# Selective scan in a four-layer token tower: the D*xc term moved to TensorE, four side jobs moved from VectorE to GpSimd and ScalarE

## The reference, cut to what matters

```
xc    = silu(conv(x_in) + conv_b)                       # 128 channels x 1024 steps
sel   = xc @ sel_w.T  ->  dt_in, Bm (16), Cm (16)
dt    = softplus(dt_in @ dt_w.T + dt_b)
dA_n  = exp(dt * A_n)          dBu_n = dt * xc * Bm_n
h_n   = dA_n * h_n(previous step) + dBu_n               # a scan along the 1024 steps
y     = sum over n of (h_n * Cm_n)  +  D * xc
out   = (y * silu(z)) @ out_w.T
```

## Time and profile before

| | |
|---|---|
| the profiled execution's own time | 1573.16 us |
| its span, first to last instruction | 1571.4 us |
| median of three runs | 1578.91 us |
| mean granted TensorE clock | 0.959 of full speed |
| TensorE busy | 1370.2 us, 87% |
| VectorE busy | 1079.3 us, 69% |
| ScalarE busy | 689.0 us, 44% |
| GpSimd busy | 415.8 us, 26% |

### The profile page before, as it was taken

One profiled execution on the slowest core, in us unless ns is written; L12 is line 12 of the kernel. 1 busy time (PEld: TensorE's weight loads), 2 busy tenths in 40 slices (PEclk: granted clock), 3 DMA queues, 4 the chain that ended last, 5 costly groups with the idle time before them and its releaser, 6 DMA issues. The chain is left out here.

```text
span 1571.4 us, 16757 instructions
## 1 busy us (share of the span) xinstructions
PE 1370.2 (87%) x5750; PEld 564.0 (36%) x5770; DVE 1079.3 (69%) x1253; ACT 689.0 (44%) x979; POOL 415.8 (26%) x242
## 2 busy tenths in 40 slices
PE   6877899988987779999997778999999777899897
PEld 2222233346422223325632222332563222333265
DVE  3598956674559995667455998556746699765673
ACT  0455543334245554324425554532541655543344
POOL 3256610012006660002100766000300276500040
PEclk9989999998999999999898999999989899999997
DMA  8100020000000002000000000200000000020000
GB/s 255 72 0 1 1 57 11 1 1 1 14 0 0 1 1 67 2 1 1 1 14 0 0 1 0 68 1 1 1 1 14 0 0 1 4 51 1 0 2 14
DMA packets 24692, 26.02 MB, mean 17 GB/s; under 512 B 4610, under 2 KB 21794, under 8 KB 24098
## 3 DMA queue, kind: packets, MB, share of 16 engines
q1 hardware_dynamic: 24002, 20.61, 4.5%
q10 hardware_dynamic: 608, 4.34, 0.9%
HBM read 20.73 MB, written 4.21 MB: 16 GB/s over the span
## 5 line engine op out<-in xcount | busy, mean ns | idle before, releaser
L405 POOL TENSOR_TENSOR scratch<-scratch 128x1024 f32<-128x1024 f32 x124 | 306.1, 2468 | 467.3 <-ACT scratch L872 312.1
L1081 DVE TENSOR_TENSOR_SCAN scratch<-ps,scratch 128x1024 f32<-128x1024 f32 x128 | 292.2, 2283 | 5.5 <-ACT ps L865 5.5
L551 PE MATMUL ps<-scratch,consts 128*128 128x512 f32 x512 | 255.6, 622 | 14.0 <-ACT work L896 12.0
L416 POOL TENSOR_TENSOR work<-work,rmax 128x512 f32<-128x512 f32 x64 | 67.4, 1053 | 614.3 <-DVE rmax L1231 614.3
L865 ACT ACTIVATE ps<-steps,vec 128x1024 f32<-128x1024 f32 x128 | 143.1, 1118 | 183.4 <-DVE scratch L1081 183.4
L1133 DVE TENSOR_TENSOR scratch<-scratch,ps 128x1024 f32<-128x1024 f32 x108 | 131.9, 1221 | 117.8 <-PE ps L610 114.8
L905 ACT ACTIVATE scratch<-ps 128x1024 f32<-128x1024 f32 x108 | 108.8, 1022 | 177.3 <-PE ps L597 177.3
L1073 DVE TENSOR_TENSOR scratch<-steps,ps 128x1024 f32<-128x1024 f32 x128 | 156.1, 1219 | 24.4 <-PE ps L525 16.3
L525 PE MATMUL ps<-bc,pick 128*128 128x512 bf16 x244 | 78.7, 402 | 98.6 <-DVE scratch L1073 97.5
L597 PE MATMUL ps<-h_odd,w 64*128 64x512 f32 x512 | 141.6, 639 | 3.8 <-ACT scratch L905 3.8
L610 PE MATMUL ps<-scratch,w 64*128 64x512 f32 x512 | 134.9, 602 | 8.1 <-DVE scratch L1133 8.1
(11 more groups left out here) (194 smaller groups left out, 1626.9 us busy)
## 6 DMA issues: line engine op xcount, KB each, us to landing
steps<-routed_table SPq DMA_DIRECT2D x128, 64.5 KB, 1.9
decayT<-in_decayT SPq DMA_DIRECT2D x8, 512.0 KB, 19.3
work<-in_table ACTq DMA_DIRECT2D x1, 2064.0 KB, 12.6
routed_table<-work SPq DMA_DIRECT2D x1, 2064.0 KB, 8.1
w<-in_w ACTq DMA_DIRECT2D x4, 512.0 KB, 19.5
out<-h_even SPq DMA_DIRECT2D x4, 512.0 KB, 2.6
bc<-in_x_next SPq DMA_DIRECT2D x3, 512.0 KB, 3.6
bc<-in_x_first SPq DMA_DIRECT2D x1, 512.0 KB, 4.5
```

The source lines that it names most:

```text
L405: pool.tensor_tensor(hc_slot(k), hs_slot(k), c_slot(k), ALU.mult).then_inc(sem["hc_ready"], 1)
L551: m = mm(ps[:, 6 + c, :], ident, hc_slot(k)[:, c * CH:(c + 1) * CH], start=(n == 0), stop=(n == NS - 1))
L1081: dve.tensor_tensor_scan(hs_slot(k), banks(DA_BANK), dbu_slot(k), 0.0, ALU.mult, ALU.add).then_inc(sem["scanned"], 1)
```

## The change

- A matrix `skip` = diag(D) is made once (VectorE, before the first pair). TensorE opens the sum of each batch with skip * xc in place of starting it with the first product; the sums then all accumulate.
- L1108 and L1120, which added D*xc, are gone, and with them the semaphore `y_read`. The final gating of batch two (L1123) reads the sum straight from PSUM.
- The gating of batch one is one GpSimd instruction of 128x1024 behind its product of unit 22, in place of two of VectorE.
- dt of batch two is added on GpSimd, piece by piece, each piece right ahead of the u that needs it.
- The middle part of batch two's split is a ScalarE copy behind copy_c(1), with a new semaphore `mid_late` that VectorE's two split_low wait for. The two split_low stay on VectorE between scans.

```diff
@@ -39,13 +39,10 @@
-MIDDLE_LATE = 3
 LOW_LATE = (5, 7)
-DT_LATE = (4, 6, 8, 10)
 U_LATE = (7, 9, 11, 13)
-Y_LATE = (NS + 4, NS + 6)
-Y_GATED = (NS + 8, NS + 10)
+Y_GATED = NS + 6
 K_SPLIT = 3
@@ -59,9 +56,9 @@
     xin_ps=NC, z_ps=NC, z_ready=2 * NC, xc_ready=2 * NC, sel_ps=2, dt_ps=2, sel_hi=2, sel_read=2, sel_split=1 + NC,
-    dt_read=2, dt_exp=2, dt_ln=2, dt_ready=1, dt_late=NN, u_ready=1, u_late=NN,
+    dt_read=2, dt_exp=2, dt_ln=2, dt_ready=1, dt_late=NN, mid_late=1, u_ready=1, u_late=NN,
     b_ps=2 * NS, c_ps=2 * NS, dA_ready=2 * NS, c_sb=2 * NS, dbu_ready=2 * NS, scanned=2 * NS, hc_ready=2 * NS + 1,
-    y_summed=2 * NS + 1, y_copied=1, y_read=2 * NC, gated_y=2 * NC,
+    y_summed=2 * NS + 1, y_copied=1, gated_y=1 + NC,
@@ -94,6 +91,7 @@
         padded = ctx.enter_context(nc.semaphore("padded"))
+        skip_ready = ctx.enter_context(nc.semaphore("skip_ready"))
         conv_folded = ctx.enter_context(nc.semaphore("conv_folded"))
@@ -112,6 +110,7 @@
         in_z = sb("in_z", [P, E])
+        skip = sb("skip", [P, E])
@@ -262,6 +261,9 @@
+
+        def rest_of(g):
+            return scratch[:, 6] if g == 0 else y_sum
@@ -394,6 +396,9 @@
                             cols = slice(c * NCH, (c + 1) * NCH)
+                            pool.wait_ge(sem["dt_ln"], at(pair, "dt_ln", 2))
+                            pool.tensor_tensor(dt[:, 1, cols], dt_pos(1)[:, cols], dt_neg(1)[:, cols],
+                                               ALU.add).then_inc(sem["dt_late"], 1)
                             pool.wait_ge(sem["dt_late"], at(pair, "dt_late", c + 1))
@@ -403,6 +408,9 @@
                             pool.tensor_tensor(hc_slot(k), hs_slot(k), c_slot(k), ALU.mult).then_inc(sem["hc_ready"], 1)
+                        if k == Y_GATED:
+                            pool.wait_ge(sem["y_copied"], at(pair, "y_copied", 1))
+                            pool.tensor_tensor(u[:, 0, :], y_sum, zs[:, 0, :], ALU.mult).then_inc(sem["gated_y"], 1)
@@ -544,12 +552,15 @@
                             pe.wait_ge(sem["y_copied"], at(pair, "y_copied", 1))
+                        pe.wait_ge(skip_ready, 1)
+                        for c in range(NC):
+                            mm(ps[:, 6 + c, :], skip[:, :], xc[:, g, c * CH:(c + 1) * CH], start=True, stop=False)
                     for c in range(NC):
...
                         m = mm(ps[:, 6 + c, :], ident, hc_slot(k)[:, c * CH:(c + 1) * CH],
-                               start=(n == 0), stop=(n == NS - 1))
+                               start=False, stop=(n == NS - 1))
                     m.then_inc(sem["y_summed"], 1)
@@ -568,12 +579,12 @@
                 pe.wait_ge(out_centred, SUM_STEPS + 2)
-                pe.wait_ge(sem["gated_y"], at(pair, "gated_y", NC))
+                pe.wait_ge(sem["gated_y"], at(pair, "gated_y", 1))
                 for c in range(NC):
...
                 for c in range(NC):
-                    pe.wait_ge(sem["gated_y"], at(pair, "gated_y", NC + 1 + c))
+                    pe.wait_ge(sem["gated_y"], at(pair, "gated_y", 2 + c))
                     mm(ps[D:P, c, :], out_wT, u[:, 1, c * CH:(c + 1) * CH], start=False, stop=True,
@@ -884,6 +895,8 @@
                 copy_c(1)
+                act.wait_ge(sem["sel_read"], at(pair, "sel_read", 2))
+                act.activation(bc[D:P, 1, :], rest_of(1)[D:P], ACT.Copy).then_inc(sem["mid_late"], 1)
                 for k in range(2, 2 * NS):
@@ -982,6 +995,7 @@
             dve.tensor_copy(ident_bf[:, :], ident)
+            dve.tensor_scalar(skip[:, :], ident, v("D"), None, ALU.mult).then_inc(skip_ready, 1)
             for pair in range(PAIRS):
@@ -1038,9 +1052,6 @@
-                def rest_of(g):
-                    return scratch[:, 6] if g == 0 else y_sum
-
@@ -1089,38 +1100,14 @@
                     scan(k)
-                    if k == MIDDLE_LATE:
-                        split_middle(1)
                     if k in LOW_LATE:
                         c = LOW_LATE.index(k)
+                        dve.wait_ge(sem["mid_late"], at(pair, "mid_late", 1))
                         split_low(1, slice(c * CH, (c + 1) * CH))
-                    if k in DT_LATE:
-                        c = DT_LATE.index(k)
-                        cols = slice(c * NCH, (c + 1) * NCH)
-                        dve.wait_ge(sem["dt_ln"], at(pair, "dt_ln", 2))
-                        dve.tensor_tensor(dt[:, 1, cols], dt_pos(1)[:, cols], dt_neg(1)[:, cols],
-                                          ALU.add).then_inc(sem["dt_late"], 1)
-
-                    if k in Y_LATE:
-                        c = Y_LATE.index(k)
-                        cols = slice(c * CH, (c + 1) * CH)
-                        dve.wait_ge(sem["y_copied"], at(pair, "y_copied", 1))
-                        dve.scalar_tensor_tensor(out=u[:, 0, cols], in0=xc[:, 0, cols], scalar=v("D"),
-                                                 in1=y_sum[:, cols], op0=ALU.mult, op1=ALU.add)\
-                           .then_inc(sem["y_read"], 1)
-                    if k in Y_GATED:
-                        c = Y_GATED.index(k)
-                        cols = slice(c * CH, (c + 1) * CH)
-                        dve.wait_ge(sem["y_read"], at(pair, "y_read", c + 1))
-                        dve.tensor_tensor(u[:, 0, cols], u[:, 0, cols], zs[:, 0, cols], ALU.mult)\
-                           .then_inc(sem["gated_y"], 1)
                 for c in range(NC):
...
                     dve.wait_ge(sem["y_summed"], at(pair, "y_summed", 2 * NS + c))
-                    dve.scalar_tensor_tensor(out=u[:, 1, cols], in0=xc[:, 1, cols], scalar=v("D"),
-                                             in1=ps[:, 6 + c, :], op0=ALU.mult, op1=ALU.add).then_inc(sem["y_read"], 1)
-                    dve.wait_ge(sem["y_read"], at(pair, "y_read", NC + 1 + c))
-                    dve.tensor_tensor(u[:, 1, cols], u[:, 1, cols], zs[:, 1, cols], ALU.mult)\
+                    dve.tensor_tensor(u[:, 1, cols], ps[:, 6 + c, :], zs[:, 1, cols], ALU.mult)\
                        .then_inc(sem["gated_y"], 1)
@@ -1264,7 +1251,7 @@
 ACT_CHAIN = 16
-DVE_CHAIN = 32
+DVE_CHAIN = 31
```

## The result

The changed kernel takes 1581.56 us (median of 20 runs); the kernel before took 1575.81 beside it (20 runs). The ratio is 1.0031, 95% interval [1.0019, 1.0042]: a little slower, where the forecast sum was 1.2 us faster. The ratio leaves out one much longer run of each kernel (1757.39 and 4255.88 us). The profiled execution takes 1581.86 us, 8.7 more than that of before.

What follows compares the result with a forecast made beforehand. VectorE was taken to set the scan stage's pace, 3.52 us per free step. Terms -11.5 - 1.1 + 7.9 + 2.3 + 1.2 = -1.2 us gave 1572.0 against the profiled 1573.16, 1577.7 on the median's scale; range 1569 to 1586.

Steps and rivals of the forecast that it cites:

- Side jobs: Between scans: middle part, dt, D*xc and gating leave VectorE, 2.88 us a pair, -11.5 us in four pairs.
- the meeting: Behind scan 7: VectorE's low part is held by GpSimd's u piece, 0.3 us a pair, +1.2 us in all.
- End of the pair: Last gating comes earlier, but ScalarE's squares limit the gain to 0.27 us a pair, -1.1 us in all.
- Opening of batch two: Two added matmuls ahead of the next spread of B delay drive and scans, partly at half clock; +7.9 us.
- Rival A: Opening of batch two: low clock lasts through all eight passes, 16.6 us in place of 7.9, net +7.5; chance 0.18.
- Opening of batch one: Same matmuls ahead of batch one's first sum, priced at 1.86 us, mostly covered by waiting time; +2.3 us.
- ScalarE's copy: Middle part on ScalarE: a copy of about 1 us fits into 1.58 us idle before decay(2); cost 0.
- GpSimd's queue: dt and gating on GpSimd delay some products by 0.3 to 1.2 us, without reaching the scans; cost 0.
- rival C: GpSimd backs up and its delays reach the scans, 2.4 us a pair, net +8.4, 1587.3 us; chance 0.08.
- B: Clock stays up at the opening of batch two, which costs 0.1 us a pair; net -8.7, 1570.2 us; chance 0.17.

Runs made afterwards that it cites:

- e9: Kernel after plus a useless VectorE job of 1.20 us behind scan 26 of each pair; 1570.44 us in its one run.
- e1: Kernel before with only the skip passes in place of VectorE's D*xc, nothing else moved; ratio 1.0013 to the kernel before.
- e2: Kernel after with D*xc back on VectorE and GpSimd's gating two units later; ratio 0.9928 to the kernel before.
- e3: Kernel after with the skip passes moved from the openings to ahead of sums 6 and 8; ratio 0.9899 to the kernel before.
- e13: Kernel after with the same useless 1.20 us VectorE job as e9, timed again with more runs; ratio 0.9976 to the kernel before.
- e4: Kernel after with ScalarE's copy of y_sum ahead of decay(18) in place of behind it; ratio 0.9856 to the kernel before.
- e7: Kernel after unaltered, profiled once more; 17.1 us from the logits to the first expert product in all pairs.

## Why the prediction was wrong

- **Side jobs, -11.5 and +1.2 for the meeting.** Measured -10.9 together, forecast -10.3. Right; the meeting cost 0.23 a pair where 0.3 was taken, on VectorE's side. The Trainium skill, SBUF — State Buffer, "Who interferes with whom", says that the two exclude each other and that the order of issue decides which one blocks. The trace agrees on who waits: the piece came first. It does not show a full block: 0.37 us of the piece were left, and the low part took 0.23 longer. (The product of 2.86 in the earlier trace rows met the middle part, a cast with one input; behind the low part, which has two, the kernel before has 2.85.)
- **End of the pair, -1.1.** Measured -1.5. ScalarE's four squares now follow one another (596.72, 1.21 for four), so 0.38 a pair was to be had.
- **Opening of batch two, +7.9: a step that failed.** It stood on "If it rises at the same time again", that the new passes take the slow place and the old ones run at full clock. The wait of 4.6 came in the first pair of the kernel after and in all pairs of e9 (4.66); in the other three pairs of after the clock fell earlier and rose later, and the wait was 5.54 to 5.66. Measured +10.0, 2.1 more: 1.3 in the first pair, where 2.3 was forecast, and 2.7 to 3.0 in the others, where 1.86 was. Rival A, by which all eight passes are slow, would have made it 16.6; the truth lies between, nearer to the forecast. By the prediction's own words 0.3 us a pair on the low level turns the sign; it was 0.5.
- **Opening of batch one, +2.3: the same step.** Measured +3.9: the four skip passes were priced at 1.86, from a sum that ran at full clock, and took 2.1 to 3.2, with the clock still low when they came. In e9 they take 1.92, and the opening costs 0.1 a pair.
- **What had no term, and weighs as much as both openings: the start of the expert block.** Here the prediction failed too. It asked only of the scan stage whether the clock falls, and left all that lies behind at nothing without giving a reason. In the kernel after four passes outside it ran at about half clock (0.51 in the window shown) in every pair, +5.1 against the first execution of before, +3.4 against the second. Without it 0.8 would be left of the 4.2 against that second execution, and 3.6 of the 8.7 against the first.
- **Range and noise.** The prediction held that within 0.5% a measurement cannot tell this kernel from no change; twenty runs of each told 0.31% with an interval of 0.12% to either side. That 1581.56 lies between its 1569 and 1586 is luck: the two are 17 us apart, and the forecast between them was for less time, not more.
- **ScalarE's copy and GpSimd's queue, 0.** Right: decay(2) still has 0.50 of idle time behind the copy, and no scan waits for a product; rival C did not come, nor did B.

Shown: the openings take the gain back (e1, e2, e3), and time alone, with no pass moved, changes the level in which the same passes run (e9 and e13 against the kernel after, and the pairs of e4 among themselves). The Trainium skill, TensorE: Matmul & The Clock Gate, "Part 1: The HAM clock gate", says that a phase of the chip decides how many matmuls run slow; the delays agree, but the pattern of a schedule also came again in a second execution (e7, 17.1 in all pairs). The four pairs of an execution follow each other at nearly one distance (389.0 to 389.2 us between their first expert products in the kernel after), so they are not four independent trials. Open: what sets that time, and why the openings of one program differ between two executions.

## What to carry to other kernels

Work added behind a wait that has idled TensorE is paid at whatever clock that idle time has left (here 3.75 us for four passes that take 1.9 at full clock); put it where TensorE has slack, or shorten the gap itself: the early copy, no part of the change, was worth 0.75% alone. When an edit shifts the rest of the program by a microsecond, look at every stretch where TensorE is lightly used, not only at the edited one. Read a difference of half a per cent by stages, and with a useless delay as a control, before the edit is called good or bad.

## What was not expected of the hardware

A useless job of 1.2 us in each pair made the kernel faster: ratio 0.9976 with it, 1.0031 without. The same two fp32 matmuls of 128x512, four passes, took from 1.96 to 3.66 us at the start of the expert block, by when they came. And a VectorE job of 0.69 us that meets a GpSimd piece of 0.73 takes 0.92, while behind it GpSimd's product takes 2.81 in place of 2.36.
